# Splitting the fused query weights on GpSimd from a raw copy in SBUF, with per-piece waits for the last weight and a new order of all queues

## The chip, the cores and the metric

One core of a Trainium2 chip runs the kernel. The metric is the time of one execution on the device in microseconds; the figure for the kernel before is the median of three runs. The core's engines work side by side: TensorE (matmuls, PE in the profile, PEld for its weight loads), VectorE (DVE), ScalarE (ACT), GpSimd (POOL), and SyncE (SP), which issues nearly all DMAs. Each engine has a queue of its own that runs strictly in order; semaphores tie the queues together.

## The reference

Two layers, each a cross attention and a feed-forward, over x of 4 batches x 256 tokens x 256 and a context of 4 x 256 x 128, in float32:

```python
x = x + _L0_xattn_ref(_layernorm(x), ctx, Wq, bq, Wk, bk)      # softmax(energy) over 256 context rows, mixes x itself
x = x + _L0_ffn_ref(_layernorm(x), w_norm, w_gv, w_out)        # 8-bit activations, ternary weights, hidden 1024
x = x + _L1_xattn_ref(_layernorm(x), ctx, mask, Wq, Wk, Wv, Wo)  # 16 heads of 128, 8 key/value heads
x = x + _L1_ffn_ref(_layernorm(x), gate_w, up_w, down_w, ...)  # weights rounded to fp8, inner 768
# within _L1_xattn_ref:
q = (text_hidden @ Wq)...;  k = (vision_tokens @ Wk)...;  v = (vision_tokens @ Wv)...
scores = jnp.einsum('bhtd,bhsd->bhts', q, k) / scale
out = jnp.einsum('bhts,bhsd->bhtd', attn, v) ... @ Wo
```

The kernel never forms k. As q k^T = x (Wq Wk^T) ctx^T, it multiplies the weights first. For each of the 8 pairs of heads (PAIRS), the fused query weight is m = Wq_head Wk^T, of 2 x 256 columns; likewise n = Wv Wo_head for the outputs.

## The kernel before

Products that need float32 precision run as three fp32r matmuls: each operand is split into a high part (the value rounded to fp32r) and a low part (value minus high part), and `product` adds high x high, high x low and low x high. So every operand exists as a pair: m_hi and m_lo, n_hi and n_lo, xT_hi and xT_lo, q_hi and q_lo, pT_hi and pT_lo (tp_lo), oT_hi and oT_lo.

The stages, in TensorE's helpers. First layer, by batch b: `project1`, `rows1`, `energy`, `probs`, `mix`. First feed-forward: `integers`, then for token tile j in two halves `gate_half` and `value_half` (the wide matmuls, line 2090), `hidden`, `ffn_out`. Weights of the second attention: `turn_kv` and `turn_queries` transpose the raw weights, `fuse_qk(i)` makes m of pair i in a PSUM bank, `fuse_vo(i)` makes n. Then the attention loop over n = 0 to 31 (4 batches x 8 pairs): `queries(n)` (m with the turned rows of x), `scores(n, h)`, the softmax on the other engines, the turn of the probabilities (`probs4` on TensorE for n = 0 to 2, 30 and 31; a VectorE block transpose and two DMAs through DRAM for the rest), `contexts(n, c)` and `attn_out(n, h)`. Last feed-forward: `rows4`, `gate4(c)`, `up4(c)`, `down(c, n)`. Work of neighbouring stages is interleaved.

Around the change: `fuse_qk(i)` writes m of pair i to a bank. ScalarE's `fused_queries(i)` (line 923) copies it, rounded, to m_hi. VectorE's `m_low(i)` (line 1502) subtracts m_hi from the bank and writes m_lo, which frees the bank. `queries(n)` of batch 0 waits for m_lo of its pair. n is handled another way: ScalarE's `fused_outputs(i)` (line 927) writes the bank out raw to n_raw, and GpSimd's `outputs_split(i)` (lines 638 and 640) copies it to n_hi and subtracts to n_lo. n_raw lies in n_lo's own place.

Each queue's order is a list of calls written out by hand at the end of its block; there is no loop in the program that sets it. `PASSING` gives for every use of a PSUM bank (what, number, bank) in TensorE's order; `passing` makes TensorE wait until the last user of that bank has left it, by the semaphores of `left_bank`. SyncE's list sets the order of loads: `raw(0)` is wk, `raw(1)` wv, `raw(2)` to `raw(9)` wq and wo in quarters; `raw(8)` and `raw(9)` go to the places of wk and wv and wait until those are turned. The last feed-forward's weights come in four loads (`eighth`) and are rounded to fp8 in 16 pieces by VectorE's `eighths` and GpSimd's `eighths` and `eighths_out`, which count up w8_done.

The prediction's helpers on the other engines. ScalarE: `values_high` and `context_high` (high parts of the context), `projected1`, `exps1`, `probs1`, `rows1`, `sums` and `ternary` (the first feed-forward's weights), `turned_kv`, `turned`, `transposed`, `silu_direct`, `rounded`, `exps`, `normalise`, `probs`, `queries`, `outputs`, `gate4_silu`, `gate4`. ScalarE loads a table when it changes between exp and silu. GpSimd: `base` (the residual for the feed-forward), `rows3`, `normalise` (half of the softmax division), `probs_low`, `hidden_in`, `integers`. VectorE: `second`, `third_stats`, `third_low`, `masked`, `inverse`, `turn_blocks`.

Of the kernel before, what the change touches and what calls it, by code (L numbers as in the profile page):

```python
# [23 lines left out]
def xattn_ffn_kernel(nc, x, ctxT, mask, wq0T, bq, wk0T, bk, w_norm, wgvT, woutT, wq, wk, wv, wo,  # L24
# [29 lines left out]
    with ExitStack() as ctx:  # L54
# [199 lines left out]
        PASSING = [("project", 0, 4), ("context", 0, 2), ("xn", 0, 3), ("energy", 0, 4), ("project", 1, 5), ("xn", 1, 6),  # L254
                   ("probs", 0, 7), ("energy", 1, 0), ("mean", 0, 4), ("mix", 0, 2), ("project", 2, 7), ("project", 3, 0),
                   ("kv", 0, 2), ("probs", 1, 7), ("energy", 2, 6), ("mix", 1, 7), ("energy", 3, 5), ("kv", 1, 1), ("xn", 2, 0),
                   ("kv", 2, 7), ("kv", 3, 0), ("hidden_in", 0, 4), ("mean", 1, 3), ("probs", 2, 2), ("mix", 2, 4),
                   ("gate", 0, 5), ("gate", 1, 2), ("gate", 2, 7), ("value", 0, 1), ("value", 1, 3), ("value", 2, 5),
                   ("vo", 0, 0), ("probs", 3, 7), ("gate", 3, 3), ("xn", 3, 0), ("value", 3, 2), ("turn", 0, 3), ("vo", 1, 7),
                   ("gate", 4, 6), ("turn", 1, 1), ("vo", 2, 0), ("value", 4, 4), ("turn", 2, 5), ("qk", 0, 6), ("qk", 1, 3),  # L260
                   ("gate", 5, 1), ("vo", 3, 2), ("gate", 6, 4), ("hidden", 0, 1), ("hidden", 1, 0), ("out", 0, 5),
                   ("out", 1, 0), ("turn", 3, 4), ("value", 5, 7), ("vo", 4, 2), ("gate", 7, 5), ("mix", 3, 1), ("turn", 4, 5),
# [2485 lines left out]
```

## Time and profile before

| | us |
|---|---|
| median of 3 runs | 319.15 |
| lowest, highest | 318.28, 320.42 |
| profiled execution, its own time | 319.45 |
| its span in the trace | 317.4 |

The span runs from the first to the last instruction of the profiled execution; its own time holds some 2 us around it. A busy TensorE is not one at its peak: the ends of its matmuls are modelled, and a matmul's listed length overlaps the next one's. The space from one start to the next shows what a matmul costs in a row of them.

### The profile page before, as it was taken

The numbers are of one execution on the slowest core, as the hardware profiler recorded it, in microseconds if no ns is written. First come the engines' busy times: TensorE is split into PE (matmuls) and PEld (weight loads), VectorE is DVE, ScalarE is ACT, GpSimd is POOL, SyncE is SP. The second block draws the span as 40 slices with busy tenths as digits, with TensorE's granted clock in tenths as the row PEclk, the third lists the DMA queues.
The fourth block names the chain that finished last, engine by engine and source line by source line (L and its number), as shares of the span: only waits on it lengthen the run. The fifth ranks groups of instructions, "written<-read, shape, count | busy, mean of one in ns | idle before, by whom it ended". The sixth has DMA issues, their size and how long they took to land.

```text
span 317.4 us, 6401 instructions
## 1 busy us (share of the span) xinstructions
PE 294.9 (93%) x1981; PEld 258.8 (82%) x1992; DVE 252.2 (79%) x713; ACT 258.5 (81%) x607; POOL 217.9 (69%) x290
## 2 busy tenths in 40 slices
PE   3676999999999999999989999999999999999994
PEld 2465566889988987899779989889999998989784
DVE  3789698989888789888889788897877595766674
ACT  0869796489999989999997897788899998975350
POOL 3786663566887788797877897878897696772001
PEclk9999799999999999999999999999999999999999
DMA  7994602002046867678637566687665466200201
GB/s 219 380 350 135 176 0 68 1 1 76 5 81 179 245 168 199 165 209 202 180 88 207 150 179 162 165 221 203 147 188 151 116 197 200 69 2 0 68 1 66
DMA packets 54609, 44.59 MB, mean 140 GB/s; under 512 B 11696, under 2 KB 45104, under 8 KB 54576
## 3 DMA queue, kind: packets, MB, share of 16 engines
q1 hardware_dynamic: 54016, 43.93, 49.1%
q8 instruction: 16, 0.26, 0.4%
q10 hardware_dynamic: 560, 0.26, 0.3%
q14 instruction: 17, 0.14, 0.1%
HBM read 27.01 MB, written 15.20 MB: 133 GB/s over the span
## 4 chain that ended last, share of the span: by engine, by line
PE 21%; ACT 15%; POOL 8%; issue 5%; DVE 1%; ACTq 0%; POOLq 0%; DVEq 0%
PE pb L2015 14%; PE pb L2278 4%; ACT sm L980 4%; POOL tp_lo L666 4%; ACT pT_hi L992 3%; PE pb L2312 2%; POOL xn L588 1%; ACT sm L998 1%; ACT L980 1%; POOL sm L661 1%; ACT L1019 1%; ACT fuse L1019 1%; ACT q_hi L975 1%; ACT oT_hi L1004 1%; POOL rstd L582 1%
## 5 line engine op out<-in xcount | busy, mean ns | idle before, releaser
L666 POOL TENSOR_TENSOR tp_lo<-tp,pT_hi 128x512 fp32r<-128x512 f32 x54 | 69.2, 1297 | 20.9 <-ACT pT_hi L992 20.8
L980 ACT ACTIVATE sm<-sm,smin 128x256 f32<-128x256 f32 x128 | 63.6, 503 | 1.1 <-DVE smin L1563 0.7
L1563 DVE CUSTOM_DVE_ANT_0 sm<-pb,mask_all 128x256 f32<-128x256 f32 x128 | 47.5, 419 | 4.0 <-PE pb L2015 3.6
L1580 DVE STREAM_TRANSPOSE blocks<-sm 128x1024 f32<-128x1024 f32 x27 | 33.5, 1240 | 7.0 <-DMA block_room<-blocks 6.1
L2015 PE MATMUL pb<-ctx_hi,q_hi 128*128 128x256 f32 x128 | 37.8, 295 | 0.5 <-DVE q_lo L1550 0.4
L2015 PE MATMUL pb<-xT_hi,m_hi 128*128 128x256 f32 x128 | 37.2, 291 | 0.1
L2015 PE MATMUL pb<-n_hi,oT_hi 128*128 128x256 f32 x128 | 37.1, 290 | 0.1
L2015 PE MATMUL pb<-xT_hi,m_lo 128*128 128x256 f32 x128 | 36.2, 283 | 0.0
L2015 PE MATMUL pb<-xT_lo,m_hi 128*128 128x256 f32 x128 | 36.2, 283 | 0.0
L2015 PE MATMUL pb<-ctx_hi,q_lo 128*128 128x256 f32 x128 | 36.2, 282 | 0.0
L2015 PE MATMUL pb<-ctx_lo,q_hi 128*128 128x256 f32 x128 | 36.1, 282 | 0.0
L2015 PE MATMUL pb<-n_lo,oT_hi 128*128 128x256 f32 x128 | 36.1, 282 | 0.0
L2015 PE MATMUL pb<-n_hi,oT_lo 128*128 128x256 f32 x128 | 36.1, 282 | 0.0
L661 POOL TENSOR_SCALAR sm<-sm,srec 128x256 f32<-128x256 f32 x64 | 30.4, 488 | 8.3 <-DVE srec L1569 8.2
L992 ACT ACTIVATE pT_hi<-tp 128x512 fp32r<-128x512 f32 x54 | 32.2, 623 | 3.4 <-PE pb L2015 3.2
L2015 PE MATMUL pb<-pT_hi,cr_hi 128*128 128x512 f32 x64 | 27.1, 424 | 2.3 <-POOL tp_lo L666 1.6
L998 ACT ACTIVATE sm<-sm,srec 128x256 f32<-128x256 f32 x64 | 28.6, 504 | 0.7 <-DVE srec L1569 0.7
L582 POOL TENSOR_TENSOR rstd<-ve,nhalf 128x2 f32<-128x2 f32 (+1 forms) x16 | 13.3, 834 | 20.1 <-DVE ve L1412 17.4
L1594 DVE TENSOR_TENSOR oT_lo<-pb,oT_hi 128x512 fp32r<-128x512 f32 x32 | 21.7, 681 | 6.0 <-ACT oT_hi L1004 5.9
L2015 PEld LDWEIGHTS pb<-ctx_hi,q_hi 128*128 128x128 f32 x128 | 24.4, 190 | 2.4 <-DVE q_lo L1550 0.9
L2015 PEld LDWEIGHTS pb<-n_hi,oT_hi 128*128 128x128 f32 x128 | 24.4, 191 | 1.4 <-DVE oT_lo L1594 0.5
L975 ACT ACTIVATE q_hi<-pb 128x512 fp32r<-128x512 f32 x32 | 18.8, 588 | 8.0 <-PE pb L2015 7.9
(195 smaller groups left out, 946.4 us busy)
## 6 DMA issues: line engine op xcount, KB each, us to landing
block_room<-blocks SPq DMA_DIRECT2D x108, 128.0 KB, 2.5
tp<-block_room SPq DMA_DIRECT2D x54, 256.0 KB, 3.1
w_raw<-in_w SPq DMA_DIRECT2D x4, 576.0 KB, 4.2
wraw<-in_wgvT SPq DMA_DIRECT2D x4, 512.0 KB, 7.4
wraw<-in_woutT SPq DMA_DIRECT2D x2, 512.0 KB, 10.6
out<-xb SPq DMA_DIRECT2D x4, 256.0 KB, 2.2
xa<-in_x SPq DMA_DIRECT2D x3, 256.0 KB, 4.6
xb<-in_ctxT SPq DMA_DIRECT2D x2, 256.0 KB, 6.1
```

The costliest lines, as they stand in the source:

```text
L582: g.tensor_tensor(rstd[:, planes, tiles(b)], ve[:, planes, tiles(b)], nhalf[:, planes, tiles(b)], ALU.pow).then_inc(rstd_done, 1)
L661: g.tensor_scalar(sm[:, n % 2, k, :], sm[:, n % 2, k, :], srec[:, n % 2, k:k + 1], 1.0, ALU.mult, ALU.mult).then_inc(norm_done, 1)
L666: g.tensor_tensor(tp_lo[:, z, c, :], tp[:, z, c, :], as_f32(pT_hi[:, c, :]), ALU.subtract).then_inc(pT_lo_pool, 1)
L975: a.activation(q_hi[:], bank(passing_bank("q", n)), ACT.Copy, scale=-SCALE).then_inc(q_hi_done, 1)
L980: a.activation(sm[:, n % 2, k, :], sm[:, n % 2, k, :], ACT.Exp, bias=smin[:, n % 2, k:k + 1], scale=-1.0, accum_out=ssum[:, n % 2, k:k + 1 ...
L992: a.activation(pT_hi[:, c, :], whole, ACT.Copy).then_inc(pT_hi_done, 1)
L998: a.activation(sm[:, n % 2, k, :], sm[:, n % 2, k, :], ACT.Identity, scale=srec[:, n % 2, k:k + 1]).then_inc(norm_act, 1)
L1563: v.tensor_tensor_reduce(out=sm[:, n % 2, k, :], in0=bank(passing_bank("s", 2 * n + h))[:, (k % 2) * S:(k % 2 + 1) * S], in1=mask_all[:, b ...
L1580: v.transpose(blocks[:].rearrange("p g k b -> p k g b"), sm[:, n % 2, :, :].rearrange("p k (g b) -> p k g b", b=32)).then_inc(blocks_done, 1)
L1594: v.tensor_tensor(oT_lo[:, n % 2, :], bank(passing_bank("ctx", n)), as_f32(oT_hi[:, n % 2, :]), ALU.subtract).then_inc(oT_lo_done, 1)
L2015: last = t_.matmul(dst, a_, b_, start=start and k == 0, stop=stop and k == n - 1, skip_group_check=check)
L2278: last = t_.matmul(dst, weight[:, k, i * P:(i + 1) * P], part[:, k, tok], start=n == 0, stop=n == 2 * KD - 1)
```

## The change

The fused query weights are treated as n is. A tile m_raw is laid over m_lo's place; ScalarE writes the bank there unrounded and thereby frees the bank; GpSimd's new `queries_split(i)` copies to m_hi and then subtracts, writing m_lo over m_raw. VectorE's `m_low` is gone. In `down`, the wait for all 16 rounded pieces before the first product of the second column half becomes a wait, for each c of the first six, for as many pieces as its slice of the weight needs. Two semaphores of the identity's set-up become one. All five queues and the list of banks are put in a new order; of that the excerpt shows the parts that the text speaks of.

```diff
+        with ExitStack() as unsplit:
+            tile(unsplit, "m_hi_room", [P, PAIRS, KD, 2 * P])
+            m_raw = tile(unsplit, "m_raw", [P, PAIRS, KD, 2 * P])
         m_hi = tile(ctx, "m_hi", [P, PAIRS, KD, 2 * P], F32R)
         m_lo = tile(ctx, "m_lo", [P, PAIRS, KD, 2 * P], F32R)
...
-                    "turn": (turned_done, 5 + n), "qk": (m_lo_done, n + 1), "vo": (n_raw_done, n + 1),
+                    "turn": (turned_done, 5 + n), "qk": (m_raw_done, n + 1), "vo": (n_raw_done, n + 1),
...
+            def queries_split(i):
+                pool.wait_ge(m_raw_done, i + 1)
+                g.tensor_copy(m_hi[:, i, :, :], m_raw[:, i, :, :]).then_inc(m_hi_done, 1)
+                pool.wait_ge(m_hi_done, i + 1)
+                g.tensor_tensor(m_lo[:, i, :, :], m_raw[:, i, :, :], as_f32(m_hi[:, i, :, :]), ALU.subtract).then_inc(m_lo_done, 1)
...
             def fused_queries(i):
                 act.wait_ge(fused_qk_ps, i + 1)
-                a.activation(m_hi[:, i, :, :], bank(passing_bank("qk", i)).rearrange("p (k n) -> p k n", k=KD), ACT.Copy).then_inc(m_hi_done, 1)
+                a.activation(m_raw[:, i, :, :], bank(passing_bank("qk", i)).rearrange("p (k n) -> p k n", k=KD), ACT.Copy).then_inc(m_raw_done, 1)
...
-            def m_low(i):
-                dve.wait_ge(m_hi_done, i + 1)
-                v.tensor_tensor(m_lo[:, i, :, :], bank(passing_bank("qk", i)).rearrange("p (k n) -> p k n", k=KD), as_f32(m_hi[:, i, :, :]),
-                                ALU.subtract).then_inc(m_lo_done, 1)
...
             def down(c, n):
                 h, i = divmod(c, KI)
                 pe.wait_ge(f_lo_done, c + 1)
+                if c < KI:
+                    pe.wait_ge(w8_done, -(-(2 * KD * INNER + (i + 1) * D) // PIECE))
                 if c == 0 and n == 0:
-                    pe.wait_ge(w8_done, B * EIGHTS)
```

The new lists, as far as the text follows them:

```
SyncE, loads after rows(3): gate_value 1, 0, 3 (2 stands ahead of rows(3)), hidden_out(0), raw(6), contexts(1), raw(2),
  norm_weight, raw(3), raw(1), hidden_out(1), mask_bytes, raw(5), raw(4), raw(0), turn_rows(1), raw(8), raw(7), raw(9)
  before: raw(0), ..., raw(4), raw(5), raw(6), raw(1), hidden_out(1), raw(3), raw(8), ...
TensorE, start: turn_context(0), project1(0), rows1(0), energy(0), rows1(1), project1(1), probs(0), energy(1), weight_sum(0),
  mix(0), project1(2), project1(3), rows1(2), probs(1), energy(2), rows1(3), mix(1), turn_kv(0), turn_kv(1), energy(3),
  weight_sum(1), probs(2), integers(0), mix(2), value_half(0, 0), gate_half(0, 0), ...
TensorE, on: ... ffn_out(1), fuse_vo(2), turn_queries(2), (3), (4), gate_half(3, 1), turn_queries(5), fuse_vo(3), rows3(0),
  fuse_vo(4), queries(0), fuse_qk(2), queries(1), turn_queries(6), scores(0), fuse_qk(3), fuse_qk(4), scores(1, 0),
  queries(2), ..., fuse_qk(5), (6), (7), queries(3), probs4(0), ...
ScalarE, start: values_high(0), projected1(0), exps1(0), sums(0), projected1(1), sums(1), probs1(0), rows1(0), exps1(1),
  rows1(1), projected1(2), projected1(3), probs1(1), exps1(2), sums(2), ternary(0), rows1(2), rows1(3), context_high(0),
  ternary(1), (2), (3), turned_kv(0), probs1(2), transposed(0), exps1(3), ...
  before: projected1(0), context_high(0), values_high(0), rows1(0), exps1(0), ..., exps1(2), ternary(2), sums(2),
  rows1(2), turned_kv(0), (1), (2), transposed(0), ternary(3), probs1(2), ...
GpSimd, middle: outputs_split(0), integers(0), ternary_out(4), (5), integers(1), queries_split(0), (1), outputs_split(1),
  rows3(0), outputs_split(2), base(2), queries_split(2), (3), outputs_split(3), queries_split(4), base(3), normalise(0),
  queries_split(5), normalise(1), queries_split(6), (7), hidden_in(2), eighths(0), integers(2), eighths_out(0), normalise(2), ...
```

## Rows read from the trace of the kernel before

**Rows 1.** Part 1 of the page: busy us, share of the span, instructions:

```profile
PE 294.9 (93%) x1981; PEld 258.8 (82%) x1992; DVE 252.2 (79%) x713; ACT 258.5 (81%) x607; POOL 217.9 (69%) x290
```

**Rows 2.** Windows: busy us (count) of PE, PEld, DVE, ACT, POOL; clock; DMA:

```profile
0.00:35.20 35.20, 22.35 (x108) 17.95 (x110) 26.14 (x87) 23.48 (x49) 22.78 (x41) 0.97 0.81 271
35.20:60.00 24.80, 23.82 (x140) 15.62 (x140) 20.88 (x49) 17.63 (x28) 15.42 (x19) 0.98 0.16 41
60.00:100.00 40.00, 39.38 (x297) 35.54 (x299) 35.08 (x116) 36.34 (x93) 25.59 (x39) 1.00 0.20 49
100.00:160.00 60.00, 58.53 (x418) 52.85 (x422) 50.34 (x148) 58.67 (x140) 49.18 (x62) 1.00 0.72 196
160.00:215.00 55.00, 53.18 (x382) 48.35 (x383) 47.83 (x148) 44.52 (x123) 45.83 (x59) 1.00 0.65 168
```

**Rows 3.** Timeline of TensorE to 34 us: start, us, instruction, count, idle before:

```profile
5.34 2.08 PE L2038 MATMUL pb<-xb,w 128*128 128x256 f32 x4 [5.34 <-DMA w<-in_wq0T]
...
23.35 1.97 PE L2075 MATMUL pb<-aT,xnT 128*128 128x256 f32 x8
```

**Rows 4.** The same from 32 to 96 us:

```profile
32.05 2.94 PE L2075 MATMUL pb<-aT,xnT 128*128 128x256 f32 x8 [1.78 <-ACT aT L906]
35.21 3.11 PE L2090 MATMUL pb<-wgv,hqT 128*128 128x512 bf16 x11 [0.22 <-issue]
...
44.08 0.59 PE L2090 MATMUL pb<-wgv,hqT 128*128 128x512 bf16 x2
44.51 0.60 PE L2173 MATMUL pb<-identf,wqo_second 128*128 128x128 f32 x4
...
59.32 0.36 PE L2015 MATMUL pb<-xT_hi,m_hi 128*128 128x256 f32 x1
...
75.38 1.04 PE L2226 MATMUL pb<-identf,sm 128*128 128x128 f32 x8
...
87.10 1.11 PE L2226 MATMUL pb<-identf,sm 128*128 128x128 f32 x8
```

**Rows 5.** One window of 1 us, columns as in rows 2:

```profile
33.00:34.00 1.00, 1.00 (x4) 0.74 (x3) 0.93 (x5) 0.98 (x2) 0.78 (x2) 0.50 0.92 269
```

**Rows 6.** Timeline of ScalarE, columns as in rows 3:

```profile
7.51 1.28 ACT L885 ACT_TABLE_LOAD   x1 [7.51 <-PE pb L2038]
...
12.00 0.47 ACT L899 ACTIVATE pr<-pb,emax 128x256 f32<-128x256 f32 x1 [0.87 <-DVE emax L1421]
...
24.85 0.48 ACT L899 ACTIVATE pr<-pb,emax 128x256 f32<-128x256 f32 x1
...
30.31 1.21 ACT L932 ACTIVATE wgv<-wraw,minus_round 128x1024 bf16<-128x1024 f32 x1
31.35 0.66 ACT L906 ACTIVATE aT<-pb 128x512 f32<-128x512 f32 x1
...
67.24 1.28 ACT L980 ACT_TABLE_LOAD   x1
```

**Rows 7.** Timeline of SyncE, which issues the DMAs:

```profile
15.16 1.98 SPq L415 DMA_DIRECT2D wqo_first<-in_wo  x1
```

**Rows 8.** DMA view of that issue: count, size, us from issue to landing:

```profile
wqo_first<-in_wo SPq DMA_DIRECT2D x1, 512.0 KB, 12.3
```

**Rows 9.** Tile m_lo, VectorE: count, ns min/median/max, first and last start:

```profile
L1502 DVE TENSOR_TENSOR m_lo<-pb,m_hi x8: 657/680/692, 56.3 to 84.5; 128x512 fp32r<-128x512 f32 x8
```

**Rows 10.** Tile n_hi, GpSimd, columns as in rows 9:

```profile
L638 POOL CAST n_hi<-n_raw x8: 609/610/619, 43.5 to 115.8; 128x512 fp32r<-128x512 f32 x8
L640 POOL TENSOR_TENSOR n_lo<-n_raw,n_hi x8: 1276/1290/1807, 44.2 to 116.5; 128x512 fp32r<-128x512 f32 x8
```

**Rows 11.** Timeline of GpSimd from 36 to 100 us, columns as in rows 3:

```profile
66.31 1.09 POOL L627 TENSOR_SCALAR xb<-xa,hfac,hadd 128x256 f32<-128x256 f32 x2 [6.41 <-PE pb L2157]
...
84.42 0.93 POOL L661 TENSOR_SCALAR sm<-sm,srec 128x256 f32<-128x256 f32 x2
...
98.60 0.93 POOL L661 TENSOR_SCALAR sm<-sm,srec 128x256 f32<-128x256 f32 x2 [1.82 <-DVE srec L1569]
```

More of the change, by code:

```diff
@@ L251, in xattn_ffn_kernel @@
         ABS_ACT, ABS_DVE = (1, 3, 5), (0, 2, 4)
[L254 to L262, printed above, removed]
[7 rows of a table removed]
-                   ("gate", 10, 0), ("s", 13, 7), ("q", 7, 1), ("gate", 11, 3), ("rows", 1, 2), ("ctx", 3, 0), ("s", 14, 3),
-                   ("s", 15, 4), ("q", 8, 5), ("q", 9, 2), ("q", 10, 4), ("s", 16, 7), ("s", 17, 1), ("ctx", 4, 7),
-                   ("s", 18, 1), ("s", 19, 2), ("value", 9, 1), ("ctx", 5, 5), ("value", 10, 2), ("value", 11, 0), ("s", 20, 3),
[3 rows of a table removed]
-                   ("s", 29, 7), ("out", 4, 0), ("out", 5, 2), ("ctx", 10, 3), ("value", 12, 0), ("rows", 2, 5), ("s", 30, 4),
[16 rows of a table removed]
@@ L2328, in _ @@
             project1(3)
-            turn_kv(0)
+            rows1(2)
             probs(1)
             energy(2)
+            rows1(3)
             mix(1)
+            turn_kv(0)
+            turn_kv(1)
             energy(3)
-            turn_kv(1)
-            rows1(2)
+            weight_sum(1)
+            probs(2)
+            integers(0)
+            mix(2)
+            value_half(0, 0)
+            gate_half(0, 0)
+            value_half(0, 1)
+            gate_half(0, 1)
+            gate_half(1, 0)
@@ L2353, in _ @@
-            turn_queries(0)
             fuse_vo(1)
             gate_half(2, 0)
+            probs(3)
+            gate_half(2, 1)
+            turn_queries(0)
             turn_queries(1)
-            fuse_vo(2)
             value_half(2, 0)
-            turn_queries(2)
+            hidden(0)
+            mix(3)
             fuse_qk(0)
             fuse_qk(1)
-            gate_half(2, 1)
-            fuse_vo(3)
             gate_half(3, 0)
-            hidden(0)
             hidden(1)
             ffn_out(0)
+            value_half(2, 1)
@@ L2368, in _ @@
+            turn_context(1)
             ffn_out(1)
+            fuse_vo(2)
+            turn_queries(2)
             turn_queries(3)
-            value_half(2, 1)
-            fuse_vo(4)
-            gate_half(3, 1)
-            mix(3)
-            turn_queries(4)
-            rows3(0)
-            fuse_vo(5)
+            turn_queries(4)
+            gate_half(3, 1)
+            turn_queries(5)
+            fuse_vo(3)
+            rows3(0)
+            fuse_vo(4)
+            queries(0)
             fuse_qk(2)
-            queries(0)
@@ L2379, in _ @@
-            turn_queries(5)
             queries(1)
+            turn_queries(6)
             scores(0, 0)
             scores(0, 1)
+            fuse_qk(3)
+            fuse_qk(4)
+            scores(1, 0)
+            queries(2)
+            value_half(3, 0)
+            scores(1, 1)
+            value_half(3, 1)
+            fuse_vo(5)
             fuse_vo(6)
-            turn_queries(6)
-            turn_context(1)
             turn_queries(7)
-            scores(1, 0)
-            scores(1, 1)
@@ L2397, in _ @@
             fuse_qk(7)
+            queries(3)
             probs4(0, 0)
```

863 lines of the change are left out of this document (432 added, 431 removed), and 47 rows, old and new, of the table PASSING.

## The prediction

> **What bounds the kernel.** The page's first part comes first: TensorE is busy 294.9 of 317.4 us [rows 1], so 22.5 us of idle time are all that any order of work can give back. The windows say where they lie [rows 2]: 12.9 us before 35.2 us, 1.0 from there to 60, 0.6 to 100, 1.5 to 160, 1.8 to 215, and the rest in the last 100 us, most of it after the last matmul, while the last bank is scaled and stored. Between 100 and 160 us ScalarE is busy 58.67 of 60 us [rows 2]: there it and TensorE limit together, so a lead or a lag that ScalarE has when the attention loop starts is carried through. The waits and the timelines then name the start-up's links: TensorE begins at 5.34 us, the first wide matmul of the first feed-forward starts at 35.21, the first query product at 59.32, the first turned probabilities at 75.38, the third pair at 87.10 [rows 3, 4]. I use these as milestones.
>
> **The split itself.** VectorE loses eight subtractions of 680 ns, 5.4 us between 56 and 85 us [rows 9]. ScalarE keeps eight copies of the same size out of PSUM, only to another tile: nothing. GpSimd gains eight copies and eight subtractions; n_hi and n_lo are the same shapes on the same engine, 610 and 1290 ns [rows 10], so 8 x 1.90 = 15.2 us. A piece is ready 1.90 us after ScalarE's copy instead of 0.68 us, 1.2 us later. Whether that is hidden depends on who asks for m_lo: queries(i) on TensorE, in order i. In the new TensorE order fuse_qk(0) and (1) stand well ahead of queries(0), and fuse_qk(2), (3), (4) each stand at least one whole product group ahead of their queries, so the 1.2 us are covered by some 1.4 to 4 us of matmuls. If that cover were gone, each of the eight would cost up to 1.2 us, 9.8 in all.
>
> Does GpSimd have the room? From 35.2 to 100 us it is busy 15.42 + 25.59 = 41.0 of 64.8 us [rows 2], and one hole of it is the 6.41 us in which base(2) waits for turn_context(1) [rows 11], which the new order moves ahead of the product groups. With 15.2 us more it is at 56.2 of 64.8. I add its new queue up. rows3(0) ends at 55.9 us, then outputs_split(2), base(2), queries_split(2), which can't start before ScalarE's copy at 63.3, queries_split(3), outputs_split(3), queries_split(4), base(3): normalise(0) starts at 73.5. With two splits, normalise(1), two more splits, hidden_in(2), eighths(0), integers(2), eighths_out(0) behind it, normalise(2) starts at 86.8 instead of 84.42 [rows 11] and ends at 87.7. TensorE asks for it at 88.35 (below): 0.65 us to spare. normalise(5) comes at 98.7 where it came at 98.60, after 1.82 us of idle time [rows 11]; there the queue has caught up.
>
> **The start, reordered.** Every queue is reordered, and this is where most of the sum lies.
> - ScalarE's first job becomes values_high(0), and turn_context(0) goes ahead of project1(0). Now the table load waits for the projection and starts at 7.51 [rows 6]; then it starts at about 5.95 and lies under the projection. With context_high(0) and rows1(0) out of the way too, exps1(0) starts at about 10.8, not 12.00 [rows 6]. Following batch 0 and 1 through, mix(1) runs at 21.85 instead of 23.35 [rows 3], and exps1(2) starts at 22.95 instead of 24.85 [rows 6].
> - From exps1(2) to the copy of the turned probabilities of batch 2, ScalarE now takes 31.35 - 24.85 = 6.5 us [rows 6]. The new list between the two has two ternary copies more (1.1 each, [rows 6]), rows1(3) and context_high(0) (0.5 each), and two turned_kv and transposed(0) less (1.6): 8.1 us. So that copy starts at 31.05 to 31.3 and mix(2) at 31.8.
> - raw(0), the key weights, is now the seventh big load, not the first. The last of six landed at 15.16 + 12.3 = 27.5 us [rows 7, 8]; loads that queue up land some 1.35 us apart, so raw(0) lands at about 28.9, and turn_kv(0), which stands ahead of energy(3) and all of batch 2, holds TensorE up from 23.7 to 28.9 us. It then does turn_kv(0), (1), energy(3), weight_sum(1), and reaches probs(2) at 30.8, about when ScalarE is ready. The 5 us are lost twice over, not added: ScalarE decides. mix(2) ends, and the wide matmuls start, at 33.65 instead of 35.21: 1.55 us earlier.
> - TensorE's clock is at 0.50, its lower level of 1.2 GHz, from 33 to 36 us (one of the three windows stands in [rows 5]), after a wait of 1.78 us just before [rows 4]. mix(2) took 2.94 us where mix(1) took 1.97 [rows 3, 4]. With a pause of 5 us ahead of it I expect such a stretch again, a little earlier, so I count no gain.
>
> **From there to the loop.** Between the first wide matmul and queries(0) stood 22.2 us of TensorE work, which took 24.1 [rows 4] (added up from start to start in the timeline; a half of the wide matmuls, for one, takes 44.51 - 44.08 = 0.43 us [rows 4], and 14 of them stand there); now it is 21.6 (turn_kv(2), (3), turn_queries(5) and turn_context(1) come in; rows1(3), fuse_vo(5) and fuse_qk(2) go out). Packed it ends at 55.3. But ffn_out(1) ends at 51.8, and the chain behind it, second(1), third_stats(0), rows3(0) on GpSimd, TensorE, ScalarE, third_low(0), takes 6.1 us and has 4.8 us of matmuls beside it. queries(0) starts at 57.9, 1.4 us earlier than 59.32, with 0.9 us less work done: 0.5 ahead. ScalarE reaches exps(0, 0), whose table load stood at 67.24 [rows 6], at about 66.0, with the same list done (turned(6), ahead of fused_queries(2), costs it a wait until 62.3): 1.2 ahead. At probs4(0, 0) TensorE is at 76.35, but with queries(3), 1.43 us, done already: 0.5 ahead of 75.38. At probs4(2, 0) it is at 88.35 with 1.4 us more done than at 87.10 [rows 4]: 0.2 ahead; ScalarE at exps(2) is 0.75 ahead. In the loop ScalarE's lead counts for most, so I take **0.8 us gained**, between the 0.2 and the 1.2.
>
> **The loop and the end.** The totals of TensorE, ScalarE and its table loads (16 by the lists, before and after) stay. ScalarE's last load moves from gate4_silu(5), where it was hidden, to gate4(6): hidden if it runs ahead of the wait, as at 33.42, or up to 1.28 us if behind it, as the load at 7.51 [rows 6]; TensorE has three other halves of a gate and up pair to do there, so 0.3 us at most. The per-piece waits of down ask for pieces 12 to 16 one by one; the last piece is done by then in either order, and eighths(15) now stands ahead of rows4(2) on GpSimd, in a hole: nothing either way.
>
> **Sum.** 317.4 - 0.8 = 316.6 us of span. The profiled execution's own time was 319.45, 2.05 above its span and 0.3 above the median of 319.15. From the median: 319.15 - 0.8 = 318.3.
>
> **Rivals.**
> 1. GpSimd becomes late (slower). One n_lo took 1807 ns where the median is 1290 [rows 10]. If all eight new subtractions stretch so, normalise(2) comes 8 x 0.52 = 4.1 us later; the 0.65 to spare taken off, TensorE loses 3.5 and the sum is +2.7: 321.9. It decides once GpSimd has slipped by over 0.65 us at normalise(2). Against it: seven of eight n_lo ran at 1.29. The Trainium skill (SBUF — State Buffer, Who interferes with whom) says that a VectorE instruction with two SBUF inputs, or in a 2-port mode, and a GpSimd instruction that reads SBUF block each other in full; by that rule the removed m_lo, with one input in PSUM, never blocked anyone, and its 16 replacements can. The trace's one long n_lo agrees with it.
> 2. The stalls go (faster). The new order may take half of the 3.3 us that TensorE idles between 100 and 215 us [rows 2], VectorE having 5 us less to do, and the clock may stay up, which by mix(2) and the eleven wide matmuls cost 1.0 + 0.5 us: 0.8 + 1.6 + 1.5 = 3.9, 315.2. For it: the loop's waits are one-off, not structural. Against: no step I can follow removes them.
> 3. The loads decide. If raw(0) lands later than 29.4 us, every microsecond is a microsecond at mix(2). Two more loads' worth, 2.7 us: 320.5. This also stands for the split being neutral while the reorder costs.
>
> **Chances.** My sum 0.55 (317.0 to 319.8), rival 1 0.15, rival 2 0.22, rival 3 0.08. A run of this kernel can tell 1%, 3.2 us, from no change. Over 1% faster is below 315.96: most of rival 2 and a tail of the sum, 0.22. Slower is above 322.34: half of rival 1 and the tail of 3, 0.13. Within: 0.65. The range of 8 in 10 is 315.0 to 321.6.
>
> **What would show it.** Eight copies and eight subtractions of m on GpSimd at 0.61 and 1.29; TensorE idle until raw(0) at about 28.9; wide matmuls from about 33.7; queries(0) near 57.9; the table load of exps(0, 0) near 66; normalise(2) near 86.8. A gap of TensorE at probs4(2) put down to GpSimd's sm would speak for rival 1, a wait at turn_kv(0) past 29.4 for rival 3, a clock of 1.00 throughout for rival 2.

## The result, and the profile after

| | before | after |
|---|---|---|
| median | 319.78 us (318.28 to 321.5, 4 runs) | 328.33 us (327.78 to 329.31, 4 runs) |
| profiled execution: time, span | 319.45, 317.4 | 327.78, 326.0 |

After over before is 1.027, with a 95% interval of 1.021 to 1.033: 8.6 us slower, where 318.3 us and a range up to 321.6 were forecast. A few executions of the experiments ran in a slower state of the core or far above the rest, and all medians and ratios below leave them out.

Part 1 of the page of the changed kernel, to be held against [rows 1]:

```profile
PE 295.7 (91%) x1981; PEld 259.0 (79%) x1992; DVE 251.9 (77%) x705; ACT 259.6 (80%) x607; POOL 234.8 (72%) x306
```

TensorE does the same work in a span 8.6 us longer. GpSimd has 16 instructions and 16.9 us more. VectorE has lost 5.4 us of instructions and is only 0.3 us less busy: others have become longer (the last section shows one line of them).

The same five windows as in [rows 2], columns as there:

```profile
0.00:35.20 35.20, 21.85 (x102) 17.53 (x103) 25.75 (x79) 21.64 (x47) 22.90 (x40) 0.95 0.74 250
35.20:60.00 24.80, 22.81 (x140) 15.11 (x140) 20.86 (x49) 19.06 (x31) 19.27 (x22) 1.00 0.23 70
60.00:100.00 40.00, 37.40 (x267) 32.95 (x269) 31.00 (x101) 31.96 (x79) 32.12 (x45) 1.00 0.17 32
100.00:160.00 60.00, 55.82 (x398) 49.57 (x400) 48.46 (x145) 57.52 (x145) 47.73 (x61) 1.00 0.66 181
160.00:215.00 55.00, 52.23 (x379) 47.76 (x380) 45.46 (x138) 45.27 (x117) 45.10 (x59) 1.00 0.66 174
```

TensorE idles more in every window: 1.0 us between 35.2 and 60, 2.0 to 100, 2.7 to 160, 1.0 to 215. There is no one gap.

To compare kernels whose orders differ I use TensorE's **lag**: the start of an item minus the packed length of all TensorE items ahead of it in its list. The packed lengths are distances from start to start in the timelines where nothing waits (a queries 1.43 us, a scores 0.72, a contexts 0.70, half of a wide product 0.43, and so on). A lag at half clock counts too. In us:

| TensorE at | before | after |
|---|---|---|
| mix(2) | 15.6 | 17.8 |
| first wide matmul of gate_half(0,0) | 16.9 | 18.0 |
| queries(0) | 18.9 | 21.4 |
| probs4(2,0), 87.10 before, 93.30 after | 19.1 | 23.9 |
| contexts(9,0), 146.28 and 154.60 | 21.9 | 30.2 |
| down(6,1), 307.49 and 315.28 | 27.9 | 35.6 |

So the changed kernel loses 1.1 us up to the first wide matmul, 3.7 more up to probs4(2,0), 3.5 more up to contexts(9,0), and gains 0.6 back behind it. The remaining 0.8 us of the span lie behind the last matmul: the last store landed 2.9 us after its issue and not 2.2. That is no work of the new order; in split_empty below, which has the old tail, it took 3.1.

The 1.1 us of the start need care. In the profiled execution of the kernel before, mix(2) and the first wide matmuls ran at half clock (2.94 us for mix(2), a granted clock of 0.50 from 33 to 36 us); in cut145, split_empty and cut36 below, with the same start, mix(2) took some 1 us less. cut36 is at value_half(0,0) by the account of the lag 1.9 us ahead of the changed kernel, so the new start costs nearer to 2 us than to 1.

TensorE's timeline (columns as in [rows 3]) shows the milestones and some of the waits:

```profile
28.87 1.48 PE L2154 MATMUL pb<-identf,stage 128*128 128x128 f32 x8 [3.32 <-DMA stage<-in_wk]
30.14 1.92 PE L2061 MATMUL pb<-qk 128*128 128x256 f32 x4
...
33.89 1.96 PE L2080 MATMUL pb<-aT,xnT 128*128 128x256 f32 x8 [0.34 <-ACT aT L924]
35.91 1.46 PE L2095 MATMUL pb<-wgv,hqT 128*128 128x512 bf16 x6
...
45.65 0.63 PE L2178 MATMUL pb<-identf,wqo_first 128*128 128x128 f32 x4 [1.23 <-ACT wqo_first L933]
...
60.94 0.39 PE L2020 MATMUL pb<-xT_hi,m_hi 128*128 128x256 f32 x1 [0.55 <-DVE xT_lo L1552]
...
80.54 1.03 PE L2231 MATMUL pb<-identf,sm 128*128 128x128 f32 x8
82.40 0.36 PE L2020 MATMUL pb<-ctx_hi,q_hi 128*128 128x256 f32 x1 [0.83 <-ACT m_raw L941]
```

turn_kv(0) stands 3.32 us; turn_queries(1) 1.23, because it writes the bank of turn_queries(0) right behind it; queries(0) 0.55; scores(2,0) 0.83, because its bank is that of fuse_qk(7), which ScalarE copies only behind probs(0,0). The releasers are a DMA, ScalarE twice, and VectorE.

The view of waits from 94 to 147 us (us in total, times, longest), of which these are TensorE's three largest, adds:

```profile
PE pb L2020 <- DVE q_lo L1563: 1.4, 1, 1.4
PE pb L2095 <- DVE smin L1576: 1.0, 1, 1.0
PE pb L2095 <- DMA hqT<-xa: 0.7, 1, 0.7
```

In the kernel before, TensorE's waits of the same window are 0.4, 0.4 and 0.3 us. The first is scores(6,0), which now stands directly behind queries(6), so that TensorE waits for its own product to be copied (before, two ffn_out stood between; there the wait is 0.4 us). That the place alone makes the wait is not shown: after_mended below puts one ffn_out back between them, and the wait grows. The second is value_half(5,1), in the bank of scores(10,0).

The split itself is as it was sized. Tile m_lo, columns as in [rows 9], and GpSimd's normalise(2), against [rows 11]:

```profile
L643 POOL TENSOR_TENSOR m_lo<-m_raw,m_hi x8: 1267/1276/1297, 51.2 to 85.6; 128x512 fp32r<-128x512 f32 x8
```

```profile
91.50 1.02 POOL L671 TENSOR_SCALAR sm<-sm,srec 128x256 f32<-128x256 f32 x2
```

### The profile page after: what moved, and what is told of

It reads as the page before. It is cut to its first block, busy times and chain, and to the rows that moved or that the text cites. A ratio compares the mean times of both kernels' runs of the same rounds, so it can differ in the third digit from the quotient of the medians.

```text
span 326.0 us, 6420 instructions
## 1 busy us (share of the span) xinstructions
PE 295.7 (91%) x1981; PEld 259.0 (79%) x1992; DVE 251.9 (77%) x705; ACT 259.6 (80%) x607; POOL 234.8 (72%) x306
## 4 chain that ended last, share of the span: by engine, by line
PE 35%; ACT 29%; DMA 9%; POOL 9%; SPq 7%; issue 6%; DVE 3%; ACTq 0%; DVEq 0%; POOLq 0%
PE pb L2020 21%; ACT sm L998 8%; PE pb L2283 4%; ACT sm L1016 3%; DMA block_room<-blocks 3%; ACT pT_hi L1010 3%; DMA stage<-in_wk 3%; PE pb L2318 3%; ACT q_hi L993 2%; POOL tp_lo L676 2%; ACT L998 2%; SPq L419 2%; ACT oT_hi L1022 2%; POOL m_lo L643 2%; DVE blocks L1593 2%
## 5 line engine op out<-in xcount | busy, mean ns | idle before, releaser
L1016 ACT ACTIVATE sm<-sm,srec 128x256 f32<-128x256 f32 x64 | 28.9, 503 | 0.6 <-DVE srec L1582 0.6
L2020 PEld LDWEIGHTS pb<-xT_hi,m_hi 128*128 128x128 f32 x128 | 24.5, 191 | 3.3 <-DVE xT_lo L1552 1.6
L1563 DVE SCALAR_TENSOR_TENSOR q_lo<-pb,q_hi 128x512 fp32r<-128x512 f32 x32 | 21.9, 683 | 6.4 <-ACT q_hi L993 6.2
L993 ACT ACTIVATE q_hi<-pb 128x512 fp32r<-128x512 f32 x32 | 18.9, 590 | 9.7 <-PE pb L2020 9.4
```

What stands on the lines that cost most here:

```text
L993: a.activation(q_hi[:], bank(passing_bank("q", n)), ACT.Copy, scale=-SCALE).then_inc(q_hi_done, 1)
L1016: a.activation(sm[:, n % 2, k, :], sm[:, n % 2, k, :], ACT.Identity, scale=srec[:, n % 2, k:k + 1]).then_inc(norm_act, 1)
L1563: v.scalar_tensor_tensor(q_lo[:], bank(passing_bank("q", n)), -SCALE, as_f32(q_hi[:]), ALU.mult, ALU.subtract).then_inc(q_lo_done, 1)
L2020: last = t_.matmul(dst, a_, b_, start=start and k == 0, stop=stop and k == n - 1, skip_group_check=check)
```

## The experiments

Theory A: the new order of the queues costs the time, the split is covered. Theory B: the 15.2 us on GpSimd make it late. Every ratio below is to the kernel before on the same chip, with its 95% interval.

### The split alone, and the order alone

**split_only** is the kernel before with the split moved. GpSimd's list:

```diff
 integers(1)
+queries_split(0)
 rows3(0)
+queries_split(1)
 outputs_split(1)
 base(2)
+queries_split(2)
 ...
 normalise(0)
+queries_split(3)
+queries_split(4)
 outputs_split(3)
 normalise(1)
+queries_split(5)
 ...
 hidden_in(2)
+queries_split(6)
 integers(2)
+queries_split(7)
```

> The kernel before in all its orders and banks, with the split alone moved: ScalarE writes the raw piece, GpSimd splits it, the eight VectorE instructions are gone, and the eight splits stand between the old items of GpSimd's list. Theory A (the re-ordered queues cost the 8.5 us, the split is covered): within 1 us of the kernel before, 318.8 to 320.8 us on a chip where that takes 319.8. Theory B (GpSimd is made late by 8 x 1.9 us of splits): 3 to 6 us slower, with TensorE waiting for rows that GpSimd normalises.

Measured: 323.88 us, ratio 1.012 (1.007 to 1.017). Neither: the split alone costs 4.2 us. TensorE is level with the kernel before up to probs4(2,0), at 82.08 us at probs4(1,0) where it was 81.96. Then, TensorE and GpSimd of split_only, and its windows:

```profile
89.80 1.47 PE L2231 MATMUL pb<-identf,sm 128*128 128x128 f32 x7 [2.43 <-issue]
```

```profile
88.72 0.98 POOL L671 TENSOR_SCALAR sm<-sm,srec 128x256 f32<-128x256 f32 x2
```

```profile
88.00:90.00 2.00, 0.20 (x2) 0.23 (x3) 1.14 (x3) 0.36 (x2) 2.00 (x4) 1.00 0.00 0
90.00:92.00 2.00, 2.00 (x12) 2.00 (x11) 0.00 (x0) 1.33 (x4) 1.92 (x3) 0.52 0.22 45
92.00:94.00 2.00, 2.00 (x13) 2.00 (x13) 1.09 (x6) 1.35 (x6) 1.92 (x4) 0.62 0.10 21
```

The wait is put down to "issue", but it ends 0.1 us behind the end of normalise(2), which ran from 88.72 to 89.70 us and not from 84.42 [rows 11]. It is paid twice: 2.4 us of standing still, then four microseconds at a granted clock of 0.52 and 0.62. The lag is 19.4 before the wait and 23.5 behind both, at contexts(2,0), where the kernel before has 19.3.

**after_no_split** is the changed kernel with the split on ScalarE and VectorE.

```diff
-a.activation(m_raw[:, i, :, :], bank(...), ACT.Copy).then_inc(m_raw_done, 1)
+a.activation(m_hi[:, i, :, :], bank(...), ACT.Copy).then_inc(m_hi_done, 1)
 # VectorE's list: m_low(0), (1) behind centred(2); (2) to (4) among masked(0, 1), (1, 0); (5), (6) behind scaled(3); (7) behind q_low(2)
```

> The changed kernel in all its orders and banks, with the split put back: ScalarE writes the high part from the bank, VectorE the low part (680 ns, eight times), nothing of it on GpSimd. Theory A: still 326.5 to 329 us, as the changed kernel (328.3). Theory B: back to 320 to 323 us.

Measured: 334.84 us, 1.048 (1.039 to 1.057), worse than the changed kernel by 6.5 us. TensorE waits 3.7 us at queries(2), which asks for m_lo(2), and 1.9 at scores(2,0), whose bank m_lo(7) has to leave. So this is the price of where I put m_low in VectorE's list, and tells nothing about B.

### The lists cut in time

**head_before**: each engine's list follows the kernel before up to one item, and from there the changed kernel's list, less what is already done. **head_after** is the reverse.

```diff
 head_before, each list: the kernel before up to (from there, the changed kernel's)
+SyncE eighth(0) | GpSimd integers(2) | ScalarE rounded(3) | VectorE outputs_low(0) | TensorE probs4(2, 1)
 head_after: the changed kernel up to (from there, the kernel before)
+SyncE eighth(0) | GpSimd normalise(2) | ScalarE normalise(2) | VectorE q_low(4) | TensorE probs4(2, 1)
```

> The lists of all five engines follow the kernel before up to about 87 us (TensorE up to probs4(2,1), split on ScalarE and VectorE), and the changed kernel's order from there to the end, its per-piece waits of down included. By the starts in the two timelines TensorE lost 4.7 to 4.9 us before this point and 3 us behind it. Theory A: 322 to 323.5 us, 3 us above the kernel before, because the later order costs by itself. Rival A2 (the later loss only follows from the late start of the loop, not from the later order): 319 to 320.5 us. Theory B says the same as A2.

Measured: 325.38 us, 1.017 (1.011 to 1.023). The lag is 18.2 at probs4(2,0), 28.3 at contexts(9,0), 35.7 at down(6,1).

> The counterpart: the changed kernel's lists, split on GpSimd included, up to probs4(2,1) of TensorE, and the order of the kernel before from there, with one bank other than its own at the seam (scores(4,1) in bank 0). Theory A: 324 to 325.5 us, 4.8 us above the kernel before. Rival A2: 327.5 to 329 us, as the changed kernel, since what is late at the seam costs the same behind it. Theory B: as A2.

Measured: 331.95 us, 1.037 (1.032 to 1.042), 3.6 us worse than the changed kernel. TensorE stands 3.8 us at contexts(2,0), right behind the seam; its lag at contexts(3,0) is 30.9, where the changed kernel has 26.1. A seam is therefore not neutral: two lists that each fit their own partners fit badly where they meet. What a hybrid adds must be read from its lag, not only from its time. head_before says that the new order costs behind 87 us although nothing was late there (A2 and B fall), but not how much: its seam alone, gate_half(4,0) to gate_half(5,0), has 2.6 us of waits. Its lag behind the seam says more: from contexts(3,0) to contexts(9,0) it grows by 5.0 us, in the changed kernel by 4.0 and in the kernel before by 1.8. So the later part of the new order loses time of its own, with no split on GpSimd and a start that is not late.

### Where the split can stand in the old order

**split_placed** moves items of GpSimd's list in split_only.

```diff
 queries_split(5)
+outputs_split(3)
+normalise(2)
+hidden_in(2)
 eighths(0)
 eighths_out(0)
-normalise(2)
-hidden_in(2)
 queries_split(6)
 ...
 hidden_in(3)
+outputs_split(4)
```

> The split alone again, as in split_only, with six items of GpSimd's list in another order: normalise(2) and hidden_in(2) stand ahead of eighths(0) and of queries_split(6) and (7), and outputs_split(3) and (4) further back. In split_only TensorE was level with the kernel before up to 87 us, then waited 2.4 us for normalise(2) (it ran at 88.72 and not 84.42) and ran 3.5 us at half its clock. Theory A (it is the place of the splits in the queue, not their 15.2 us): normalise(2) at about 84.5, no wait, 319.3 to 320.8 us where the kernel before takes 319.8. Theory B (GpSimd has no 15 us to spare in this stretch wherever they stand): 322 to 325 us, another wait for GpSimd between 80 and 105 us.

Measured: 323.81 us, 1.014 (1.012 to 1.016). normalise(2) ran in time, at 83.04:

```profile
83.04 0.94 POOL L671 TENSOR_SCALAR sm<-sm,srec 128x256 f32<-128x256 f32 x2
```

TensorE did not wait at probs4(2,0). It waited later, between 88 and 110 us (view of waits):

```profile
DVE blocks L1593 <- POOL sm L671: 1.5, 1, 1.5
...
PE pb L2020 <- DVE q_lo L1563: 1.6, 1, 1.6
...
PE pb L2020 <- DVE oT_lo L1607: 1.1, 1, 1.1
```

GpSimd's normalise(4) was late, VectorE's turn_blocks waited for it, and q_low and outputs_low stood behind that in VectorE's queue.

**split_late** moves three more items back: `outputs_split(4)` behind `probs_low(3, 1)`, `outputs_split(5)` and `(6)` behind `normalise(6)`.

> split_placed with three more items of GpSimd moved: outputs_split(4), (5) and (6) behind probs_low(3,1), normalise(6) and each other, where their output is first needed near 120 us. In split_placed normalise(4) began at 101.56 (before: 95.85), VectorE waited for it with turn_blocks and then for its own queue, and TensorE waited 1.6 us for q_lo(6) and 1.1 us for oT_lo(2). If GpSimd's lateness between 87 and 107 us is the cause: normalise(4) at about 96, both waits at 0.5 us or none, 319.3 to 320.5 us where the kernel before takes 319.3. If GpSimd cannot hold the 15.2 us in any order: 322 us or more.

Measured: 327.32 us, 1.025 (1.021 to 1.029). Worse: the work now stands ahead of probs_low, and TensorE waits at contexts(4,0):

```profile
120.09 0.50 PE L2020 MATMUL pb<-pT_hi,cr_hi 128*128 128x512 f32 x1 [2.35 <-POOL tp_lo L676]
```

**split_empty** takes the length away and leaves the waits and places of split_only.

```diff
-g.tensor_copy(m_hi[:, i, :, :], m_raw[:, i, :, :])
+g.tensor_copy(m_lo[:, i, :, 0:8], as_f32(m_hi[:, i, :, 0:8]))
-g.tensor_tensor(m_lo[:, i, :, :], m_raw[:, i, :, :], as_f32(m_hi[:, i, :, :]), ALU.subtract)
+g.tensor_tensor(m_lo[:, i, :, 8:16], as_f32(m_hi[:, i, :, 0:8]), as_f32(m_hi[:, i, :, 8:16]), ALU.subtract)
 # ScalarE writes m_hi; TensorE reads m_hi in place of m_lo
```

> split_only (the kernel before in its own orders, split on GpSimd) with the eight splits emptied: GpSimd's two instructions run on 8 of 256 columns, ScalarE writes the piece into the high part's place, TensorE reads the high part in place of the low part. So the low part of the fused query weights is left out. If the length of the splits costs (15.2 us in a queue that has no room for it between 70 and 107 us): 318.8 to 320 us, 4 us under split_only's 323.9. If the waits and the places cost: 323 us as split_only.

Measured: 319.83 us, 1.001 (0.999 to 1.003, 12 runs). So in the old order the 4 us are the length of the splits on GpSimd, and not their waits; taking VectorE's 5.4 us away gives nothing. That the length acts through GpSimd's queue is seen at normalise(2); VectorE is 1.5 us less busy with the splits emptied (249.7 and 251.2 us), and what that is worth was not tried apart. Three placements cost 4.2, 4.5 and 8.3 us: a slip of GpSimd between 70 and 107 us comes out at another consumer each time.

### The same question in the new order

**after_empty_split** is the changed kernel with the same edit.

> The changed kernel with all its orders, banks and waits, but GpSimd's eight splits emptied: ScalarE writes the piece into the high part's place, GpSimd runs its two instructions on 8 of 256 columns, and TensorE reads the high part in place of the low part too. So the low part of the fused query weights is left out of the computation; every other instruction stays. Theory A (order costs): 326.5 to 328.3 us. Theory B (GpSimd's 15.2 us cost): 321 to 324 us.

Measured: 327.51 us, 1.026 (1.022 to 1.030), 0.8 us under the changed kernel, which the two intervals do not separate. Tile m_lo and GpSimd's timeline of this kernel:

```profile
L643 POOL TENSOR_TENSOR m_lo<-m_hi x8: 218/221/222, 52.9 to 84.4; 128x16 fp32r<-128x16 f32 x8
```

```profile
91.44 0.94 POOL L671 TENSOR_SCALAR sm<-sm,srec 128x256 f32<-128x256 f32 x2 [0.66 <-DVE srec L1582]
...
98.57 0.94 POOL L671 TENSOR_SCALAR sm<-sm,srec 128x256 f32<-128x256 f32 x2 [2.55 <-DVE srec L1582]
```

This execution's start was 1.9 us later than the changed kernel's (first wide matmul at 37.77, not 35.91), so its times can't be set side by side as they stand: normalise(2), at 91.44 and 91.50, came 1.9 us earlier against the wide matmuls with 12 us of split work gone. TensorE gained nothing by it. GpSimd now waits for VectorE there, and the lag grows by 5.8 us from the first wide matmul to probs4(2,0), as in the changed kernel (5.9; before 2.2), which has no wait at probs4(2,0) either: its normalise(2) ended 0.8 us ahead of it. In the new order the split is covered to within what the two intervals separate, and nearly all of the 8.6 us is the order's.

### Single waits of the new order, mended

**after_raw0**: SyncE's `raw(0)` ahead of `raw(6)`.

> The changed kernel with one load moved: raw(0) is issued ahead of raw(6), not behind raw(4). TensorE then finds raw(0) at turn_kv(0) by about 25.5 us and not at 28.87. If the start's wait decides: gate_half(0,0) 1 us or more earlier, 326.5 to 327.5 us. If ScalarE decides there anyway (my prediction's reading): gate_half(0,0) moves by less than 0.5 us, 328 us.

Measured: 329.19 us, 1.031 (1.027 to 1.034). TensorE of this kernel:

```profile
28.86 1.12 PE L2154 MATMUL pb<-identf,stage 128*128 128x128 f32 x8 [3.26 <-ACT xnT L910]
```

The load was issued at 6.70 us and had landed by 17.6, and turn_kv(0) stood until the same 28.86: its bank is that of rows1(2), which ScalarE copies at 28.14. That is no second cause that had been hidden in the changed kernel. There ScalarE had copied rows1(2) by 27.87, and the load, landed at 28.83, did decide. The moved load pushed another back, and ScalarE now waited for that one:

```profile
26.04 1.06 ACT L894 ACTIVATE su<-wraw 128x1024 f32<-128x1024 f32 x1 [0.76 <-DMA wraw<-in_woutT]
```

In the changed kernel it stood 0.68 us for TensorE at the copy of the turned probabilities; one wait was exchanged for another of the same size, and what the start gains without both, these runs don't show.

**after_energy**: the same, and `energy(3)` ahead of `turn_kv(0)` on TensorE.

> The changed kernel with raw(0) issued ahead of raw(6) and with energy(3) ahead of turn_kv(0) on TensorE, so that TensorE has 0.9 us of work in the 3.4 us in which turn_kv(0) waits. If TensorE's order decides the start: mix(2) 1 us or more earlier than 33.89, 327 us. If ScalarE's list decides (it copies rows1(2), whose bank turn_kv(0) wants, at 28.4 us and goes on to exps1(3)): mix(2) within 0.4 us of 33.89, no change in the time, 328.3 us.

Measured: 330.09 us, 1.031 (1.027 to 1.034). mix(2) at 33.98, as before the edit:

```profile
33.98 2.67 PE L2080 MATMUL pb<-aT,xnT 128*128 128x256 f32 x8 [2.24 <-ACT aT L924]
```

With raw(0) early, ScalarE's list sets the start (it has one wait between exps1(2) and the copy, 0.45 us for the same pushed-back load); what is handed to TensorE earlier waits there.

**after_banks**: two entries of the table of banks.

```diff
-("turn", 1, 2), ... ("value", 11, 0)
+("turn", 1, 4), ... ("value", 11, 4)
```

> The changed kernel with two PSUM banks reassigned: turn(1) to bank 4 (it shares bank 2 with turn(0) right ahead of it and TensorE waits 1.2 us for ScalarE's copy), value(11) to bank 4 (its bank 0 is that of scores(10,0), read by VectorE late; TensorE waits 1.4 us). If the banks are the cause both waits go: 325.5 to 327 us. If what is behind them is late by itself: the waits appear within a few items again, 328 us.

Measured: 328.76 us, 1.028 (1.024 to 1.032). Both waits are gone from the trace. Behind the first, hidden(0) now waits 0.6 us; behind the second the lag grows from 30.0 at contexts(5,0) to 31.2 at contexts(7,0), where it grew from 28.2 to 29.6. The profiled execution reached its first wide matmul only at 39.07 us, after waits for loads and two stretches at half clock, so only this growth can be compared.

**after_hidden6**: SyncE's `turn_hidden(6)` ahead of `blocks_written(18)`.

> The changed kernel with turn_hidden(6) ahead of blocks_written(18) in SyncE's list, where the kernel before has it. GpSimd has uq(6) ready at 198.05, the transfer is issued at 202.95 behind the block transfers of round 18, and TensorE stands at ffn_out(6) until 207.2. If SyncE's order is the cause: issue by 199, no wait at ffn_out(6), 1.6 to 1.9 us less, 326.5 us. If the loop takes its pace from elsewhere: 328.3 us.

Measured: 327.68 us, 1.026 (1.023 to 1.030). In the changed kernel SyncE's queue stood so:

```profile
199.98 1.86 SPq L445 DMA_DIRECT2D block_room<-blocks  x4
201.95 0.90 SPq L458 DMA_DIRECT2D tp<-block_room  x2
202.95 1.24 SPq L434 DMA_TRANSPOSE uqT<-uq  x1
```

with uq(6) ready since 198.1. With the edit the stop of 1.6 us at ffn_out(6) goes and one of 0.5 us at ffn_out(7) comes. The lag grows by 1.5 us from contexts(14,0) to contexts(17,0), not by 2.3.

**after_out_late**: outputs_split(4) to (6) late, as in split_late. **after_mended**: this, after_banks, after_hidden6, and `ffn_out(3)` behind `queries(6)`.

> The changed kernel with the same three items moved, outputs_split(4), (5), (6), to behind probs_low(3,1) and normalise(6). Its normalise(4) began at 102.76. If GpSimd's lateness carries the changed kernel's losses behind 87 us (scores(6,0) 1.7, contexts(5,0) 0.7, value_half(5,1) 1.4): 325 to 326.5 us. If it is the order and the banks of the others: 328 us.

Measured: 333.12 us, 1.043 (1.039 to 1.047): a stop of 3.6 us at contexts(5,0), the mechanism of split_late.

> The changed kernel with four mends at once: outputs_split(4) to (6) late as in after_out_late, turn_hidden(6) ahead of blocks_written(18), turn(1) and value(11) in bank 4, and ffn_out(3) behind queries(6), so that TensorE has work while queries(6) is copied. If each wait is one of place and they add up: 1.4 + 1.0 + 1.0 + 2 to 3 us, so 322 to 323.5 us. If a mended wait only moves to the next late engine: 326 us or more.

Measured: 330.99 us, 1.036 (1.032 to 1.039). It has the stop of 3.6 us of after_out_late at contexts(5,0) too. Against after_out_late, on the same chip, the other three mends are worth 2.1 us together; my sum, 5.4 to 6.4 us for all four, was a miss. One of the three did harm:

```profile
104.73 0.38 PE L2020 MATMUL pb<-ctx_hi,q_hi 128*128 128x256 f32 x1 [1.84 <-DVE q_lo L1563]
```

That is scores(6,0), with ffn_out(3) now between it and queries(6), and it waits 1.84 us where it waited 1.41. VectorE's list was left as it was: it reads the product of ffn_out(3) ahead of making q_lo(6), and so stood 1.47 us for TensorE until 102.93 before it came to q_lo(6) at 103.99. An item moved in one queue needs its reader moved in the other.

### The cuts at 36 and 145 us, and the waits of down

> The lists of all engines follow the kernel before up to its first wide product at 35 us (loads, start of TensorE, ScalarE, VectorE, GpSimd), and the changed kernel from there, split on GpSimd included. If the start's new order costs (TensorE lost 17.8 and not 15.6 us by mix(2)): 1 to 2 us under the changed kernel, 326.3 to 327.3 us. If the start is neutral: 328.3 us. The rest of the loss, 6 to 8 us, should stay in both readings.

```diff
 cut36: the kernel before up to (from there, the changed kernel with its split)
+SyncE raw(7) | GpSimd hidden_in(1) | ScalarE turned_kv(3) | VectorE scaled(1) | TensorE mix(2)
 cut145: the kernel before up to (from there, the changed kernel's order)
+SyncE eighth(2) | GpSimd integers(5) | ScalarE normalise(11) | VectorE outputs_low(7) | TensorE contexts(8, 1)
```

Measured: 326.81 us, 1.022 (1.018 to 1.025), 1.5 us under the changed kernel. By these medians the old start gives 1.5 us back, though the two intervals (1.021 to 1.033 for the changed kernel) overlap, and the rest of the loss stays: the lag grows by 6.1 us from the first wide matmul to probs4(2,0) and by 6.1 to contexts(9,0).

> The kernel before up to contexts(8,1) at 142 us, split on ScalarE and VectorE, and the changed kernel's order behind it, per-piece waits of down included. In the changed kernel's trace TensorE loses 1.8 us at ffn_out(6) for the hidden transfer behind the block transfers, and saves 1 us at contexts(11,1). If each stretch carries its own waits: 320 to 321 us (ffn_out(6) waits again, contexts(11,1) doesn't). If a change of order costs 3 us or more at any seam: 323 us or more.

Measured: 321.5 us, 1.006 (1.003 to 1.010, 10 runs). From 184 to 212 us (view of waits):

```profile
PE pb L2130 <- DMA uqT<-uq: 2.4, 1, 2.4
```

and a low clock behind it (0.75 from 201 to 203 us, 0.50 to 205). **cut145_hidden6** moves `turn_hidden(6)` ahead of `blocks_written(18)` in it.

> cut145 with one item moved: turn_hidden(6) ahead of blocks_written(18) in SyncE's list. In cut145 TensorE lost 4.7 us between contexts(14,0) and contexts(17,0), where the kernel before loses 1.0: it stood 2.6 us at ffn_out(6) and ran slower for 5 us after it. If this one item is the cause: the wait is under 1 us, about 3 us come back, 318.8 to 320 us. If something else is late there: 322 us.

Measured: 320.72 us, 1.0025 (1.000 to 1.005, 12 runs), 0.8 us less, which the two intervals do not separate. The lag between contexts(14,0) and contexts(17,0) grows by 3.0 and not 4.7 us: part of it was this one item. What is left there, 2 us more than in the kernel before, was a stop of 1.05 at scores(21,0) and one of 0.8 at ffn_out(7).

> The kernel before with the per-piece waits of down alone: six thresholds of w8_done in place of one, no order changed. Both theories: no change, within 0.5 us of the kernel before, since all eighths are written long before down(0,0).

Its edit is the one of the change, in `down` alone: `if c < KI: pe.wait_ge(w8_done, -(-(2 * KD * INNER + (i + 1) * D) // PIECE))`. Measured: 319.7 us, 0.999 (0.997 to 1.002, 12 runs). Nothing, as forecast.

## Why the prediction was wrong

**What bounds the kernel** held: TensorE's idle time is the whole account.

Against the forecast the profiled execution is 2.3 us late at the first wide matmul, 2.7 more at probs4(2,0), 3.5 more at contexts(9,0), and 0.6 less from there on; the 0.8 us behind the last matmul and my choice of 0.8 us gained over the 0.2 that TensorE had at probs4(2,0) make up the rest.

**The split: sizes right, cover half right.** 0.61 and 1.28 us eight times, as sized from [rows 10]. Of the room on GpSimd the new order has enough: after_empty_split gains 0.8 us, not told apart from nothing. normalise(2) came at 91.50 and not 86.8, but TensorE asked for it at 93.30 and not 88.35. In the old order there is no room: 4.2 us, and the first wait is at normalise(2), the very place of rival 1, though the trace of the kernel before has 1.75 us to spare there (84.42 + 0.93 to 87.10), and through the queue and not through stretched instructions. None of the eight subtractions took more than 1297 ns, so rival 1's mechanism did not occur on GpSimd. Stretched instructions occurred on VectorE (last section), and mostly not because of the split: with the splits emptied VectorE is nearly as busy, 251.0 us against 251.9.

**The start: one step failed, at 2.1 us.** That turn_kv(0) would hold TensorE until 28.9 was right (28.87). "ScalarE decides" was nearly right: ScalarE stood 0.68 us for TensorE, and with raw(0) early it stood about as long for another load (after_raw0, after_energy). But the term "exps1(0) at about 10.8" came out at 11.53, since the table load did not wait for the projection to hide it and turn_context(0) took the place that it freed: TensorE began at 5.81 and not 5.34, and ScalarE's copy of the projection ran at 8.74, as early as before. (Some of that is how early the first load lands in an execution: in after_banks TensorE began at 5.10 and exps1(0) ran at 10.81.) exps1(2) was at 24.29 and not 22.95, 1.3 us. And the list from there to the copy of the turned probabilities took 8.9 us, not 8.1, 0.7 of it a wait for TensorE, which did energy(3) at low clock. Together 2.1 us: mix(2) at 33.89, not 31.8. ScalarE of the changed kernel, columns as in [rows 6]:

```profile
2.20 1.28 ACT L937 ACT_TABLE_LOAD   x1 [2.20 <-issue]
6.97 0.60 ACT L937 ACTIVATE cr_hi<-pb 128x512 fp32r<-128x512 f32 x1 [3.48 <-PE pb L2162]
8.74 0.84 ACT L903 ACTIVATE qk<-pb,bqk 128x256 f32<-128x256 f32 x2 [1.18 <-PE pb L2043]
11.53 0.47 ACT L917 ACTIVATE pr<-pb,emax 128x256 f32<-128x256 f32 x1 [1.95 <-DVE emax L1439]
...
24.29 0.47 ACT L917 ACTIVATE pr<-pb,emax 128x256 f32<-128x256 f32 x1 [1.13 <-DVE emax L1439]
...
33.15 0.60 ACT L924 ACTIVATE aT<-pb 128x512 f32<-128x512 f32 x1 [0.68 <-PE pb L2069]
```

**From there to the loop: the step that counted work and not banks, 2.7 us.** I added matmuls up and let ffn_out(1) and its chain set queries(0) at 57.9; it came at 60.94. I never asked of each new neighbour which bank it writes and who has to leave it: turn_queries(1) behind turn_queries(0) in bank 2 (1.4 us of lag), scores(2,0) in the bank of fuse_qk(7) (1.0). The table load of exps(0,0) came at 69.90, not 66.0, after a copy of m(2) at 66.55, not 63.3.

**The loop and the end: the step that failed most, 3.5 us.** "The totals stay" is true, and no argument for time. From probs4(2,0) to contexts(9,0) the new order loses 6.3 us where the old one loses 2.8: the stops at scores(6,0) behind queries(6), at value_half(5,1) in the bank of scores(10,0), and others, each small. I had followed no item behind 98 us and priced the stretch at nothing. The end was right (down_pieces; 5.4 us from contexts(9,0) to down(6,1), before 6.0). Rival 3 had said in one half sentence that the split may be neutral while the reorder costs, and gave it 0.08 with a price for the loads alone.

What stays open: the new order costs some 7 us more than the old one between the first wide matmul and contexts(9,0) in the account of the lag, and the two waits that after_banks took away there did not make the kernel measurably faster. Which items carry the rest, and how much of the cuts' times is their seams, no run here settles.

## What to carry to other kernels

Where every queue is reordered, equal totals say nothing: go through the new TensorE list item by item, and ask of each which bank it takes, who leaves it and how far back its own input was made, all the way to the end of the last stage that is touched. An engine at 69% of the span can be full where the work is moved to; the cheapest test of "it has room" is to empty the moved instructions and keep their waits, in the old order and in the new. A wait that is mended in one queue may only move to the next late one, and an item moved in one list without its reader in another can make the wait longer, as ffn_out(3) did.
